# Attention on one core: casts and the normalising product read PSUM, V is made ahead of the denominators, and two of a step's four maxima move ahead of its value products

## The chip, the core and the metric

The program runs on one core of a Trainium2 chip. Its engines are TensorE (PE, matmuls; PEld is its weight load), VectorE (DVE), ScalarE (ACT) and GpSimd (POOL), with SyncE (SP) issuing DMAs; they run independently and wait for each other by semaphores. SBUF is the working memory; PSUM, where matmuls write, has 8 banks of 128 x 512 f32. The metric is the device time of one execution in microseconds; the time of a kernel is the median of its runs.

## The reference, cut to the part that is changed

The whole program is a layer norm, an attention block, a feed-forward block with two convolutions, a whitening and a state-space block, on an input of 16 images of 64 channels and 32 x 32 points. Only the attention is changed:

```python
qkv = x_ln @ w_qkv.T                              # x_ln: 16 images x 1024 points x 64
q, k, v = (to_heads(t) for t in jnp.split(qkv, 3, axis=-1))     # 8 heads of 32
scores = jnp.einsum('bhqd,bhkd->bhqk', q, k) * HEAD_DIM ** (-0.5)
attn = jax.nn.softmax(scores, axis=-1)
out = jnp.einsum('bhqk,bhkd->bhqd', attn, v)
```

## The kernel before

The attention goes through 32 periods: 16 images, each with two groups of four heads. A period has 16 steps, s = 0 to 15, in two halves of eight: the half picks 512 queries, and the step within it, kb = 0 to 7, picks 128 keys. The order on each engine is written out by hand (`period` in each engine's block), with semaphores between engines. An engine takes its own list in that order.

In a step PE makes the scores of four heads (L402, into the four banks `at_sc`) and subtracts each query's maximum with a one-row matmul (L409). ACT turns them into `at_probs` in two exponentials of two heads each (L510). PE multiplies them by V into the single bank `at_O` (`values`, L421; the table `PV_AT` says in which step which blocks are multiplied). POOL adds the probabilities up over kb (L607, five additions per half, and one block by DMA, L602), and PE turns the sums into denominators in `at_O` (`denominator`, L385). ACT takes Ln and Exp(-x) of them (`reciprocal`, L482 and L486), and DVE multiplies the raw output by that (`normalise`, L568).

The maxima for the softmax are made ahead, by a second, cheaper product of bf16 copies of q and k (`QH`, `KH`): four matmuls per step, one per head (`maxima`, L341), each into one bank of the ring `at_ring`, and DVE reduces each over its 512 keys (`reduce`, L548). The ring has three banks (`SLOTS`), dealt out in turn. A fourth kind of unit also uses the ring: `extra` says in which step q or k of the next period is projected (`project`, L354; q in steps 0 and 9, k in 1 and 3) or the maxima are turned into a row (`turn`, L379; steps 7 and 15). The unit that gets a bank waits until the one three places before it in the ring's order has been taken out (`wait_for_bank`). So the fourth maximum of a step waits for the reduction of the first of the same step, or of the second where an extra unit stands between.

For q and k, ACT takes the projection from the ring to SBUF (`take`, L469), and DVE casts that copy to bf16 (`cast`, L563), both in SBUF, after the reductions of the step. V of the next period is projected into `at_O` (`values_projected`, L369) in step kb = 3, after the reciprocal has read it, and taken by ACT (L490). The waits stand in the order in which PE meets them:

```python
scores(stage, grp, par, s)
maxima(stage, grp, par, s, (0, 1))
# kb == 2: denominators_added, denominators_sums;  kb == 3: values_projected
for k in PV_AT.get(kb, ()): ...            # values
for kind, which in extra.get(s, []): ...   # turn or project
maxima(stage, grp, par, s, (2, 3))
```

Of the kernel before, what the change touches and what calls it, by code (L numbers as in the profile page):

```python
# [11 lines left out]
P = 128  # L12
# [135 lines left out]
def attention_phase(nc, sem, xn_d, wqkvT, ident_bf, attn_d):  # L148
# [73 lines left out]
    with ExitStack() as ctx:  # L222
# [18 lines left out]
        rden = sb("at_rden", [P, HALF])  # L241
# [79 lines left out]
        def _(pe):  # L321
# [35 lines left out]
            def values_projected(stage, grp, par, half):  # L357
                if stage == "last":
                    return
                if stage == "lead" or (stage == "first" and half == 0):  # L360
                    if v_halves(grp, half) > 1:
                        pe.wait_ge(v_done, v_halves(grp, half) - 1)
                else:
                    pe.wait_ge(lden_done, 2 * grp + half)
                at = 2 * INNER + (1 - par) * P
                rows = slice(half * C, (half + 1) * C)
                for n in range(KB // 2):
                    k = half * KB // 2 + n
                    m = nc.tensor.matmul(O[:, blk(n)], xn[rows, blk(k)], w[rows, at:at + P], start=True, stop=True)  # L369
                m.then_inc(v_ready, 1)  # L370
# [17 lines left out]
            def denominators_added(of_half):  # L388
                pe.wait_ge(raw_done, of_half + 1)
# [21 lines left out]

            def values(stage, grp, par, half, kb):
                if kb == 0:
                    if stage == "last":
                        pe.wait_ge(lden_done, 2 * grp + half)
                    else:
                        pe.wait_ge(v_done, v_halves(grp, half))
                if kb == KB - 1:
                    pe.wait_ge(exp_done, 2 * (STEPS * grp + KB * half + kb) + 2)
                for h in range(GH):  # L420
                    m = nc.tensor.matmul(O[head(h), :], V[:, par, kb, head(h)], probs[:, kb, h, :],  # L421
                                         start=(kb == 0), stop=(kb == KB - 1))
                m.then_inc(pv_done, 1)
# [4 lines left out]
            def period(grp, par, stage):  # L428
                for s in range(STEPS):
                    half, kb = divmod(s, KB)  # L430
                    closes = stage != "lead" and not (stage == "first" and half == 0)
                    was_grp, was_par, was_half = half_before(grp, par, half)
                    if stage != "lead":
                        scores(stage, grp, par, s)
                    maxima(stage, grp, par, s, (0, 1))
                    if closes and kb == ADDED_AT:
                        denominators_added(2 * grp + half - 1)
                    if closes and kb == SUMS_AT:
                        denominators_sums(2 * grp + half - 1, was_half)
                    if kb == V_AT:  # L440
                        values_projected(stage, grp, par, half)
                    if stage != "lead":
# [5 lines left out]
                    for kind, which in extra.get(s, []):  # L448
                        if kind == "turn":
                            turn(stage, grp, which)  # L450
                        else:
                            project(stage, grp, par, kind, which)
                    maxima(stage, grp, par, s, (2, 3))
                if stage == "last":
                    values(stage, grp, par, 1, KB - 1)
                    denominators_added(2 * NG - 1)
                    denominators_sums(2 * NG - 1, 1)

            pe.wait_ge(xn_in, 2 * DMA)
# [4 lines left out]
        def _(act):  # L464
            nc.scalar.preload_act_table_set("natural_log_exp_and_others")

            def take(stage, grp, unit, to):
                act.wait_ge(extra_ready, unit_count(stage, grp, unit))
                nc.scalar.activation(to, ring[:, unit[3], :], ACT.Copy).then_inc(extra_done, 1)  # L469

            def take_raw(grp, half):
# [5 lines left out]
            def reciprocal(of_half):  # L477
# [6 lines left out]
                if not first:  # L484
                    act.wait_ge(od_free, of_half)
# [7 lines left out]
            def period(grp, par, stage):  # L493
                for s in range(STEPS):
# [17 lines left out]
                                                 scale=SCALE).then_inc(exp_done, 1)  # L512
                    if closes and kb == 0:
                        take_raw(grp if half else grp - 1, 1 - half)
                    if closes and kb == SUMS_AT:
                        reciprocal(2 * grp + half - 1)
                    if stage != "last" and kb == V_AT:
                        take_v(grp, par, half)
# [16 lines left out]
        def _(dve):  # L535
# [22 lines left out]
            def cast(stage, grp, par, kind, which):  # L558
                if not executed(stage, kind, which, which):
                    return  # L560
                of, to = {"q": (QT, QH), "k": (KT, KH)}[kind]
                dve.wait_ge(extra_done, unit_count(stage, grp, unit_of(stage, kind, which)))
                nc.vector.tensor_copy(to[:, 1 - par, hs(which)], of[:, 1 - par, hs(which)]).then_inc(cast_done, 1)  # L563

            def normalise(grp, half):
                dve.wait_ge(raw_done, 2 * grp + half + 1)
                dve.wait_ge(rden_done, 2 * grp + half + 1)
                nc.vector.tensor_tensor(att[:, half, :], att[:, half, :], rden[:], ALU.mult).then_inc(od_free, 1)  # L568

            def period(grp, par, stage):  # L570
                for s in range(STEPS):
                    reduce(stage, grp, s, (0, 1))
                    if s == 3 and stage not in ("lead", "first"):
                        normalise(grp - 1, 1)
                    if s == KB + 3 and stage != "lead":
                        normalise(grp, 0)
                    reduce(stage, grp, s, (2, 3))
                    for kind, which in extra.get(s, []):
                        if kind in MADE_AHEAD:
                            cast(stage, grp, par, kind, which)  # L580
                    if s == LATE - 1:
                        combine(stage, grp, s, 1)
                    if s == LATE + KB - 1:
# [1184 lines left out]
```

## Time and profile before

| | |
|---|---|
| median of 3 runs | 3789.77 us (3788.62 to 3790.57) |
| the profiled execution: its own time, its span | 3794.89 us, 3793.2 us |
| mean granted TensorE clock | 0.911 of full |
| busy of the span: PE, DVE, ACT, POOL | 86%, 73%, 54%, 60% |
| DVE reductions of the maxima (L548) | 2048, 1289.7 us |
| POOL additions of the probabilities (L607) | 320, 1451.3 us |
| ACT exponentials (L510) | 1024, 992.8 us |

The attention takes more than half of the span, and nothing outside it is changed. In its stretch PE looks busy nearly all the time, so the lengths of steps and the waits between matmuls say more than busy shares. A row of a timeline gives the start, the duration (of the whole group, if several instructions were merged), the engine, the line, what is written and read, the count, and in brackets the idle time before it and what ended it. Starts of PE rows are exact; their ends are modelled.

### The profile page before, as it was taken

Reading aid. Unit: us, or ns where it says so; the run is one execution under the profiler, and the core shown is the slowest. Engines: PE = TensorE matmul, PEld = TensorE weight load, DVE = VectorE, ACT = ScalarE, POOL = GpSimd, SP = SyncE. Lnnn points to the kernel's source line nnn. Section 1 sums busy time; section 2 is a strip of 40 time slices with the busy share of each in tenths; the row PEclk is TensorE's granted clock in tenths of the full one; section 3 lists DMA queues with packets and bytes.
Section 4 is the critical chain, followed back from the end, with each engine's and each line's share of the span. In section 5 each row is a group of like instructions: output and inputs, shape, how many; then the busy total and the mean of one; then the engine's idle time right before and its main releaser. Section 6 shows DMA issues by size and latency. Waiting matters only on the chain. (4 is left out here: it accounts for less than half of the span.)

```text
span 3793.2 us, 55116 instructions
## 1 busy us (share of the span) xinstructions
PE 3248.7 (86%) x18038; PEld 1243.0 (33%) x18038; DVE 2753.4 (73%) x3346; ACT 2046.5 (54%) x2445; POOL 2269.8 (60%) x748
## 2 busy tenths in 40 slices
PE   6999999999989999999999599955688887888887
PEld 2333333333333333333333133342222222222322
DVE  5788878888778888787885122223788888888888
ACT  3566666666656666666666233323556455455464
POOL 0677777777767777777777200001666666667666
PEclk7799999999989999999999799977898999999999
DMA  2121222122212221222212411013443344434433
GB/s 99 34 51 44 55 48 48 43 49 48 48 43 48 48 48 43 48 49 51 48 43 48 127 67 72 11 58 107 146 150 139 118 143 151 134 119 148 150 136 121
DMA packets 83956, 301.94 MB, mean 80 GB/s; under 512 B 14112, under 2 KB 15204, under 8 KB 75444
## 3 DMA queue, kind: packets, MB, share of 16 engines
q1 hardware_dynamic: 69460, 215.06, 16.9%
q0 software_dynamic: 14272, 83.94, 10.0%
q8 instruction: 135, 2.21, 0.2%
q14 instruction: 89, 0.73, 0.1%
HBM read 192.42 MB, written 39.39 MB: 61 GB/s over the span
## 5 line engine op out<-in xcount | busy, mean ns | idle before, releaser
L548 DVE TENSOR_REDUCE at_pmax<-at_ring 128x1 f32<-128x512 f32 x2048 | 1289.7, 683 | 378.7 <-PE at_ring L341 377.5
L607 POOL TENSOR_TENSOR at_prob_sums<-at_prob_sums,at_probs 128x2048 f32<-128x2048 f32 x256 | 1161.1, 4535 | 394.0 <-ACT at_probs L510 383.1
L510 ACT ACTIVATE at_probs<-at_sc 128x1024 f32<-128x1024 f32 x1024 | 992.8, 1021 | 701.1 <-PE at_sc L409 698.1
L1661 POOL TENSOR_TENSOR ss_drive<-ss_du,ss_bsb 128x1024 f32<-128x1024 f32 x261 | 610.9, 2353 | 270.9 <-DVE ss_state L1618 263.2
L402 PE MATMUL at_sc<-at_QT,at_KT 32*128 32x512 f32 x4096 | 765.4, 677 | 7.4 <-issue 5.3
L341 PE MATMUL at_ring<-at_KH,at_QH 32*128 32x512 bf16 x2048 | 490.6, 406 | 124.8 <-DVE at_pmax L548 120.6
L1561 ACT ACTIVATE ss_decay<-ss_delta,ss_a 128x512 f32<-128x512 f32 x520 | 354.4, 687 | 447.3 <-DVE ss_state L1614 301.3
L421 PE MATMUL at_O<-at_probs,at_V 128*32 128x512 f32 x4096 | 530.0, 626 | 1.1 <-ACT at_probs L510 1.1
L1450 PE MATMUL ss_Y<-ss_seen,ss_ident 128*128 128x512 f32 x1032 | 524.1, 632 | 0.0
L1626 DVE TENSOR_TENSOR ss_seen<-ss_state,ss_C 128x1024 f32<-128x1024 f32 x259 | 316.2, 1221 | 87.5 <-PE ss_C L1438 79.6
L341 PEld LDWEIGHTS at_ring<-at_KH,at_QH 32*128 32x128 bf16 x2048 | 149.0, 95 | 678.3 <-DVE at_pmax L548 445.4
L607 POOL TENSOR_TENSOR at_prob_sums<-at_probs 128x2048 f32<-128x2048 f32 x64 | 290.2, 4534 | 119.4 <-ACT at_probs L510 119.4
L1618 DVE TENSOR_TENSOR_SCAN ss_state<-ss_decay,ss_state,ss_drive 128x512 f32<-128x512 f32 x259 | 332.2, 1283 | 31.5
L1614 DVE TENSOR_TENSOR_SCAN ss_state<-ss_decay,ss_drive 128x512 f32<-128x512 f32 x259 | 314.8, 1216 | 32.4 <-POOL ss_drive L1661 16.5
L1438 PE MATMUL ss_C<-ss_bc,ss_select 96*128 96x512 bf16 x518 | 163.6, 399 | 188.9 <-DVE ss_seen L1626 188.5
L409 PE MATMUL at_sc<-at_nrow,at_ones_bf 1*128 1x512 bf16 x2048 | 307.5, 401 | 0.1
L1450 PEld LDWEIGHTS ss_Y<-ss_seen,ss_ident 128*128 128x128 f32 x1032 | 204.8, 203 | 233.0 <-issue 197.2
L402 PEld LDWEIGHTS at_sc<-at_QT,at_KT 32*128 32x128 f32 x4096 | 253.1, 194 | 21.8 <-ACT at_probs L510 11.0
L965 POOL DMA_DIRECT2D scratch_x<-fc_out x8 | 4.3, 534 | 353.4 <-ACT fc_out L866 353.4
L354 PE MATMUL at_ring<-at_xn,at_w 64*128 64x512 f32 x256 | 166.3, 742 | 31.5 <-DMA at_xn<-scratch_xn 19.6
L421 PEld LDWEIGHTS at_O<-at_probs,at_V 128*32 128x32 f32 x4096 | 103.7, 112 | 249.0 <-issue 247.0
L1438 PEld LDWEIGHTS ss_C<-ss_bc,ss_select 96*128 96x128 bf16 x518 | 40.5, 101 | 383.2 <-DVE ss_seen L1626 318.6
(196 smaller groups left out, 3069.2 us busy)
## 6 DMA issues: line engine op xcount, KB each, us to landing
ss_bsb<-scratch_rows SPq DMA_DIRECT2D x265, 512.0 KB, 7.1
at_probs<-at_probs POOLq DMA_DIRECT2D x64, 1024.0 KB, 7.0
scratch_attn<-at_att SPq DMA_DIRECT2D x64, 256.0 KB, 2.0
fc_att<-scratch_attn SPq DMA_DIRECT2D x32, 512.0 KB, 5.6
ss_xn<-scratch_xm SPq DMA_DIRECT2D x34, 256.0 KB, 5.7
at_xn<-scratch_xn SPq DMA_DIRECT2D x32, 256.0 KB, 3.8
ss_xw<-scratch_xw SPq DMA_DIRECT2D x17, 256.0 KB, 3.8
ln_x<-in_x SPq DMA_DIRECT2D x8, 512.0 KB, 4.3
```

The costliest lines, as they stand in the source:

```text
L341: nc.tensor.matmul(ring[:, unit[3], :], QH[head(h), p, blk(quad // 2)], KH[head(h), p, hs(quad % 2)], start=True, stop=True).then_inc(max_ ...
L402: nc.tensor.matmul(sc[:, h, :], KT[head(h), par, blk(kb)], QT[head(h), par, hs(half)], start=True, stop=False)
L421: m = nc.tensor.matmul(O[head(h), :], V[:, par, kb, head(h)], probs[:, kb, h, :], start=(kb == 0), stop=(kb == KB - 1))
L510: nc.scalar.activation(probs[:, kb, two, :].rearrange("p h q -> p (h q)"), sc[:, two, :].rearrange("p h q -> p (h q)"), ACT.Exp, scale=SCA ...
L548: nc.vector.tensor_reduce(pmax[:, quad // 2, h, quad % 2:quad % 2 + 1], ring[:, unit[3], :], AX_X, ALU.max, negate=True).then_inc(max_done, 1)
L607: nc.gpsimd.tensor_tensor(prob_sums[:, half, :, :], before, probs[:, k, :, :], ALU.add).then_inc(pool_sums, 1)
L1450: m = nc.tensor.matmul(Y[:, hs(h)], ident[:], seen[:, n % DEPTH, hs(h)], start=False, stop=(n == N - 1))
L1561: nc.scalar.activation(decay[:, hs(h)], delta[:, par, hs(h)], ACT.Exp, scale=a_neg[:, n:n + 1])\
L1614: nc.vector.tensor_tensor_scan(now[:, hs(0)], decay[:, hs(0)], drive[:, n % DEPTH, hs(0)], 0.0, ALU.mult, ALU.add).then_inc(first_half_don ...
L1618: nc.vector.tensor_tensor_scan(now[:, hs(1)], decay[:, hs(1)], drive[:, n % DEPTH, hs(1)], now[:, HALF - 1:HALF], ALU.mult, ALU.add).then_ ...
L1626: nc.vector.tensor_tensor(seen[:, n % DEPTH, :], state[:, n % 2, :], Cp[:], ALU.mult).then_inc(seen_done, 1)
L1661: nc.gpsimd.tensor_tensor(drive[:, n % DEPTH, :], du[:, par, :], bsb[:, n % SLOTS, :], ALU.mult).then_inc(drive_done, 1)
```

## The change

Five things are done together, all in the attention:

- `cast` reads the projection from the ring in PSUM, where it read ACT's copy in SBUF. It waits for PE alone, and stands between the reductions of heads 0 and 1 and those of heads 2 and 3 of its step. ACT's `take` of q and k now waits for the cast, so that the bank is given back after both.
- The reciprocal's Exp writes `at_O` in place of an SBUF tile `rden`, and `normalise` reads it from there. It stands ahead of all four reductions of kb = 3, where it stood between the second and the third.
- V is projected in kb = 1, right after the raw output has been taken, and the denominators of kb = 2 wait until ACT has taken V.
- The first block of value products waits for `normalise` and goes into kb = 3. `PV_AT` has 1, 2, 2, 1, 1 blocks in kb = 3 to 7, and before had 2, 2, 2, 1 in kb = 4 to 7.
- On PE, projections, turns and the maxima of heads 2 and 3 come ahead of the step's value products, where they came behind them.

```diff
-    ADDED_AT, SUMS_AT, V_AT = 2, 2, 3
+    V_AT, SUMS_AT = 1, 2
-    PV_AT = {0: (LAST_KB,), 4: (0, 1), 5: (2, 3), 6: (4, 5), 7: (6,)}
+    PV_AT = {0: (LAST_KB,), 3: (0,), 4: (1, 2), 5: (3, 4), 6: (5,), 7: (6,)}
...
-                    pe.wait_ge(lden_done, 2 * grp + half)
+                    pe.wait_ge(raw_done, 2 * grp + half)
...
-                    if stage == "last":
-                        pe.wait_ge(lden_done, 2 * grp + half)
+                    if stage == "first" and half == 0:
+                        pe.wait_ge(v_done, v_halves(grp, half))
                     else:
-                        pe.wait_ge(v_done, v_halves(grp, half))
+                        pe.wait_ge(od_free, 2 * grp + half)
...
+                if unit[1] in MADE_AHEAD:
+                    act.wait_ge(cast_done, casts(grp, *unit[1:3]))
                 nc.scalar.activation(to, ring[:, unit[3], :], ACT.Copy).then_inc(extra_done, 1)
...
-                nc.scalar.activation(rden[:], lden[:], ACT.Exp, scale=-1.0).then_inc(rden_done, 1)
+                nc.scalar.activation(O[:], lden[:], ACT.Exp, scale=-1.0).then_inc(rden_done, 1)
...
-                dve.wait_ge(extra_done, unit_count(stage, grp, unit_of(stage, kind, which)))
-                nc.vector.tensor_copy(to[:, 1 - par, hs(which)], of[:, 1 - par, hs(which)]).then_inc(cast_done, 1)
+                dve.wait_ge(extra_ready, unit_count(stage, grp, unit))
+                nc.vector.tensor_copy(to[:, 1 - par, hs(which)], ring[:, unit[3], :]).then_inc(cast_done, 1)
...
-                nc.vector.tensor_tensor(att[:, half, :], att[:, half, :], rden[:], ALU.mult).then_inc(od_free, 1)
+                nc.vector.tensor_tensor(att[:, half, :], att[:, half, :], O[:], ALU.mult).then_inc(od_free, 1)
```

On PE, a step with two blocks of value products (kb = 5), before: `at_max_done` is the reductions' semaphore, `at_cast_done` the casts', and x8 value products are two blocks of four heads.

```order
L341 MATMUL at_ring<-at_KH,at_QH 128x512 [waits at_max_done,at_cast_done]
L341 MATMUL at_ring<-at_KH,at_QH 128x512 [waits at_max_done]
L421 MATMUL at_O<-at_probs,at_V 32x512 x8
L341 MATMUL at_ring<-at_KH,at_QH 128x512 [waits at_max_done] x2
L402 MATMUL at_sc<-at_QT,at_KT 128x512 [waits at_exp_done]
```

The same place after:

```order
L340 MATMUL at_ring<-at_KH,at_QH 128x512 [waits at_max_done,at_cast_done]
L340 MATMUL at_ring<-at_KH,at_QH 128x512 [waits at_max_done] x3
L423 MATMUL at_O<-at_probs,at_V 32x512 x8
L404 MATMUL at_sc<-at_QT,at_KT 128x512 [waits at_exp_done]
L404 MATMUL at_sc<-at_QT,at_KT 128x512
```

The value products stood between the second and the third maximum; all four maxima now stand in a row ahead of them, and the next scores follow the value products.

On DVE, from the second reduction of step 0 to the cast of step 1 (the register rows set a wait's count), before:

```order
L548 TENSOR_REDUCE at_pmax<-at_ring 128x1 [waits at_max_ready]
L562 ISA
L563 CAST at_QH<-at_QT 128x512 [waits at_extra_done]
L547 REGISTER_ALU
L548 TENSOR_REDUCE at_pmax<-at_ring 128x1 [waits at_max_ready]
L547 REGISTER_ALU
L548 TENSOR_REDUCE at_pmax<-at_ring 128x1 [waits at_max_ready]
```

After:

```order
L550 TENSOR_REDUCE at_pmax<-at_ring 128x1 [waits at_max_ready]
L565 ISA
L566 CAST at_QH<-at_ring 128x512 [waits at_extra_ready]
L549 REGISTER_ALU
L550 TENSOR_REDUCE at_pmax<-at_ring 128x1 [waits at_max_ready]
L549 REGISTER_ALU
L550 TENSOR_REDUCE at_pmax<-at_ring 128x1 [waits at_max_ready]
```

The cast before follows the fourth reduction of its step and waits for ACT's copy; after, it follows the second, and waits for the projection itself.

## Rows read from the trace of the kernel before

**Rows 1.** L475 by source: instructions, shortest, median, longest ns, first and last start.

```profile
L475 ACT ACTIVATE at_att<-at_O x64: 597/597/603, 136.7 to 2090.0; 128x512 f32<-128x512 f32 x64
```

**Rows 2.** Windows: length, busy by engine (instructions), granted clock, DMA share, GB/s.

```profile
90.00:2100.00 2010.00, 1859.63 (x14278) 727.00 (x14278) 1586.26 (x2268) 1239.46 (x1466) 1504.95 (x384) 0.92 0.21 47
```

**Rows 3.** Timeline of PE, a step with two blocks of value products.

```profile
802.58 1.24 PE L402 MATMUL at_sc<-at_QT,at_KT 32*128 32x512 f32 x8
...
803.76 0.38 PE L341 MATMUL at_ring<-at_KH,at_QH 32*128 32x512 bf16 x2
804.07 1.92 PE L421 MATMUL at_O<-at_probs,at_V 128*32 128x512 f32 x16
805.92 0.39 PE L341 MATMUL at_ring<-at_KH,at_QH 32*128 32x512 bf16 x2
```

**Rows 4.** Timeline of DVE behind those maxima.

```profile
806.35 2.48 DVE L548 TENSOR_REDUCE at_pmax<-at_ring 128x1 f32<-128x512 f32 x4 [0.64 <-PE at_ring L341]
```

**Rows 5.** Timeline of PE, the one block of value products of step 8.

```profile
814.51 1.07 PE L421 MATMUL at_O<-at_probs,at_V 128*32 128x512 f32 x8
815.51 0.39 PE L341 MATMUL at_ring<-at_KH,at_QH 32*128 32x512 bf16 x2
```

**Rows 6.** Timeline of PE from the denominators of step 10 to the scores of step 13.

```profile
820.16 1.06 PE L385 MATMUL at_O<-at_probs,at_ones 128*32 128x512 f32 x8
...
822.02 0.39 PE L341 MATMUL at_ring<-at_KH,at_QH 32*128 32x512 bf16 x1
824.39 0.39 PE L341 MATMUL at_ring<-at_KH,at_QH 32*128 32x512 bf16 x1 [1.98 <-DVE at_pmax L548]
824.48 1.24 PE L402 MATMUL at_sc<-at_QT,at_KT 32*128 32x512 f32 x8
...
827.57 2.36 PE L402 MATMUL at_sc<-at_QT,at_KT 32*128 32x512 f32 x8
...
833.68 1.24 PE L402 MATMUL at_sc<-at_QT,at_KT 32*128 32x512 f32 x8
```

**Rows 7.** Timeline of DVE and of POOL: the casts and what POOL runs.

```profile
819.96 3.77 DVE L563 CAST at_QH<-at_QT 128x512 bf16<-128x512 f32 x1
823.65 3.71 DVE L548 TENSOR_REDUCE at_pmax<-at_ring 128x1 f32<-128x512 f32 x6
...
863.90 0.42 DVE L563 CAST at_KH<-at_KT 128x512 bf16<-128x512 f32 x1
...
818.91 4.53 POOL L607 TENSOR_TENSOR at_prob_sums<-at_probs 128x2048 f32<-128x2048 f32 x1 [0.38 <-ACT at_probs L510]
```

**Rows 8.** Windows of 2 us in the slow step 12.

```profile
829.00:831.00 2.00, 2.00 (x16) 0.37 (x12) 1.31 (x3) 0.89 (x1) 0.00 (x0) 0.50 0.35 131
```

**Rows 9.** Waits of 90 to 2100 us: in total, times, longest.

```profile
PE at_ring L341 <- DVE at_pmax L548: 118.3, 96, 2.0
```

**Rows 10.** Timeline of PE: V projected and a projection of q, each with its follower.

```profile
394.86 1.16 PE L369 MATMUL at_O<-at_w,at_xn 64*128 64x128 f32 x8
395.95 0.39 PE L341 MATMUL at_ring<-at_KH,at_QH 32*128 32x512 bf16 x2
...
846.61 1.12 PE L354 MATMUL at_ring<-at_xn,at_w 64*128 64x512 f32 x2
847.67 0.39 PE L341 MATMUL at_ring<-at_KH,at_QH 32*128 32x512 bf16 x2
```

**Rows 11.** Timeline of ACT: the reciprocal of step 10.

```profile
822.15 0.60 ACT L482 ACTIVATE at_lden<-at_O 128x512 f32<-128x512 f32 x1 [0.27 <-PE at_O L385]
822.78 0.63 ACT L486 ACTIVATE at_rden<-at_lden 128x512 f32<-128x512 f32 x1
```

**Rows 12.** By source, as rows 1: DVE products, and the reductions.

```profile
L568 DVE TENSOR_TENSOR at_att<-at_att,at_rden x64: 680/1367/3471, 148.0 to 2097.2; 128x512 f32<-128x512 f32 x64
L1626 DVE TENSOR_TENSOR ss_seen<-ss_state,ss_C x259: 1220/1221/1222, 2677.4 to 3787.9; 128x1024 f32<-128x1024 f32 x130
L548 DVE TENSOR_REDUCE at_pmax<-at_ring x2048: 673/681/694, 67.0 to 2049.0; 128x1 f32<-128x512 f32 x187
```

More of the change, by code:

```diff
@@ L386, in denominator, with denominators_added @@
                 return m
-            def denominators_added(of_half):
-                pe.wait_ge(raw_done, of_half + 1)
+            def denominators_added(of_half, v_count):
+                if v_count is None:
+                    pe.wait_ge(raw_done, of_half + 1)
+                else:
+                    pe.wait_ge(v_done, v_count)
                 pe.wait_ge(block_added, DMA * (of_half + 1))
@@ L435, in period @@
                     maxima(stage, grp, par, s, (0, 1))
[L436 to L439, printed above, removed]
                     if kb == V_AT:
                         values_projected(stage, grp, par, half)
+                    if closes and kb == SUMS_AT:
+                        denominators_added(2 * grp + half - 1, None if stage == "last" else v_halves(grp, half))
+                        denominators_sums(2 * grp + half - 1, was_half)
+                    for kind, which in extra.get(s, []):
+                        if kind != "turn":
+                            project(stage, grp, par, kind, which)
+                    for kind, which in extra.get(s, []):
+                        if kind == "turn":
+                            turn(stage, grp, which)
+                    maxima(stage, grp, par, s, (2, 3))
                     if stage != "lead":
@@ L447, in period @@
                                 values(stage, was_grp, was_par, was_half, k)
[L448 to L453, printed above, removed]
                 if stage == "last":
                     values(stage, grp, par, 1, KB - 1)
-                    denominators_added(2 * NG - 1)
+                    denominators_added(2 * NG - 1, None)
                     denominators_sums(2 * NG - 1, 1)
@@ L483, in reciprocal @@
                 act.wait_ge(lden_done, of_half + 1)
-                if not first:
-                    act.wait_ge(od_free, of_half)
-                nc.scalar.activation(rden[:], lden[:], ACT.Exp, scale=-1.0).then_inc(rden_done, 1)
+                nc.scalar.activation(O[:], lden[:], ACT.Exp, scale=-1.0).then_inc(rden_done, 1)
             def take_v(grp, par, half):
@@ L514, in period @@
                         take_raw(grp if half else grp - 1, 1 - half)
+                    if stage != "last" and kb == V_AT:
+                        take_v(grp, par, half)
                     if closes and kb == SUMS_AT:
                         reciprocal(2 * grp + half - 1)
-                    if stage != "last" and kb == V_AT:
-                        take_v(grp, par, half)
                     for kind, which in extra.get(s, []):
@@ L560, in cast @@
                     return
-                of, to = {"q": (QT, QH), "k": (KT, KH)}[kind]
-                dve.wait_ge(extra_done, unit_count(stage, grp, unit_of(stage, kind, which)))
-                nc.vector.tensor_copy(to[:, 1 - par, hs(which)], of[:, 1 - par, hs(which)]).then_inc(cast_done, 1)
+                to = {"q": QH, "k": KH}[kind]
+                unit = unit_of(stage, kind, which)
+                dve.wait_ge(extra_ready, unit_count(stage, grp, unit))
+                nc.vector.tensor_copy(to[:, 1 - par, hs(which)], ring[:, unit[3], :]).then_inc(cast_done, 1)
             def normalise(grp, half):
@@ L567, in normalise @@
                 dve.wait_ge(rden_done, 2 * grp + half + 1)
-                nc.vector.tensor_tensor(att[:, half, :], att[:, half, :], rden[:], ALU.mult).then_inc(od_free, 1)
+                nc.vector.tensor_tensor(att[:, half, :], att[:, half, :], O[:], ALU.mult).then_inc(od_free, 1)
             def period(grp, par, stage):
                 for s in range(STEPS):
+                    if s == SUMS_AT + 1 and stage not in ("lead", "first"):
+                        normalise(grp - 1, 1)
+                    if s == KB + SUMS_AT + 1 and stage != "lead":
+                        normalise(grp, 0)
                     reduce(stage, grp, s, (0, 1))
[L573 to L577, printed above, removed]
                     for kind, which in extra.get(s, []):
@@ L580, in period @@
                             cast(stage, grp, par, kind, which)
+                    reduce(stage, grp, s, (2, 3))
                     if s == LATE - 1:
```

1 line of the change is left out of this document (removed).

## The prediction, made before the changed kernel had run

> **What bounds the kernel now.** I read the length of a half first: ACT takes the raw output once per half, 64 times from 136.7 to 2090.0 [rows 1], so a half lasts (2090.0 - 136.7) / 63 = 31.0 us. Then the steps in PE's timeline. In an undisturbed step with two blocks of value products the scores start at 802.58, the maxima 1.18 us later, the value products 1.49 us later, and the next maxima and scores at 805.92 [rows 3]: 3.34 us, with PE never idle. DVE is through four maxima in 2.48 us and then waits for PE [rows 4]. Such steps are bound by PE.
>
> Two places per period are not. In step 10 the fourth maximum starts 1.98 us late, behind a reduction [rows 6], because DVE stood in a cast of 3.77 us [rows 7]. The same cast takes 0.42 us with POOL idle; here POOL was inside its addition of 4.53 us [rows 7]. So the cast waits for POOL, DVE for the cast, and PE for DVE. Over the attention PE waits 118 us in this way [rows 9]. Behind the long wait the granted clock falls to 0.50, the 1.2 GHz level [rows 8], and a step with two blocks takes 833.68 - 827.57 = 6.11 us [rows 6], which is 2.8 us more than 3.34. The mean clock of 0.92 over 2010 us [rows 2] makes 2 x 0.08 x 2010 = 322 us at the lower level, a loss of at most half of that, 161 us. All that the casts can give back is thus 118 + 161 = 279 us.
>
> **Casts, product and V.** The trace has no cast from PSUM. Its bounds are 0.42 and 3.77 us [rows 7]; the nearest row is the reduction of the same 512 numbers of PSUM, 0.673 to 0.694 us in all 2048 cases, POOL busy or not [rows 12]. I take 0.68, so the wait of 1.98 us goes. The Trainium skill ("VectorE: DVE Perf Modes", section "Why PSUM operands drop a tier") says that a PSUM operand costs a copy its faster mode, and its cycle table gives an estimate of (120 + 512) / 0.96 GHz = 0.66 us; no run here shows it, and with 0.66 the sum would be some 2 us lower. A cast at 0.42 us would save 0.26 us in three steps per period, some 25 us.
>
> The product took 0.68 us or, next to POOL, 1.37 [rows 12]. With one PSUM operand the nearest row is the product of the state-space block, 1.22 us for twice the columns in all 259 cases, with POOL at work beside it [rows 12]; I take 0.68. At 1.37 each half would be 0.7 us longer, 43 us in all.
>
> ACT's copy of q and k now waits for the cast, and behind it on ACT stand the next step's exponentials. In kb = 1 the projection ends 3.6 us into the step, the cast 0.7 and the copy 0.6 us later (a copy of ACT takes 0.6 us [rows 1]), 1.2 us into the next step; its scores are not complete before that, since its maxima follow them at 1.18 [rows 3]. So nothing is lost on ACT, and what the bank's late return costs on PE is counted below at kb = 1 and 2.
>
> V costs PE 395.95 - 394.86 = 1.09 us [rows 10] wherever it stands. It waits for the raw output, which ACT has taken 0.6 us [rows 1] after the last value product of kb = 0, while PE is still at the scores of kb = 1: no wait. The denominators, 822.02 - 820.16 = 1.86 us [rows 6], find V taken. SP's loads and stores wait for the same events, and POOL's order is unchanged.
>
> **The maxima ahead of the value products.** This is the term that decides. The ring has three banks, so the fourth maximum of a step waits for the reduction of the first. Before, the value products stood between and hid that. Now nothing does. From the start of a step's scores: first maximum at 1.18, over 0.38 later [rows 3]; DVE starts 0.06 later (a maximum ends at 805.92 + 0.39, DVE starts at 806.35 [rows 3, 4]); one reduction 0.68 [rows 12]; PE 0.06 later (the reduction ends at 823.65 + 0.68, the maximum starts at 824.39 [rows 6, 7]). The fourth maximum starts at 2.36. PE does not pass it: at 824.39 the scores behind it, whose own inputs were ready, started only 0.09 us after the released maximum [rows 6]. The value products come 0.31 later (804.07 - 803.76 [rows 3]), at 2.67; two blocks take 1.86 [rows 3], one block 1.00 (815.51 - 814.51 [rows 5]). Where a turn or projection stands between, the wait is for the second reduction, 0.60 later ((2.48 - 0.68) / 3 [rows 4]). New lengths of steps:
>
> - kb = 4 and 5, two blocks: 2.67 + 1.86 = 4.53 each. kb = 6, one block: 3.67. kb = 7, one block and a turn: 4.27.
> - kb = 0: 3.67, or 4.27 in the first half, with q's projection.
> - kb = 1: 1.49 + 1.09 (V) + 1.06 (projection, 847.67 - 846.61 [rows 10]) = 3.65; 0.1 more in the first half, where the bank of q comes free only after cast and take.
> - kb = 2: 1.49 + 1.86, and about 0.2 for the same reason = 3.55.
> - kb = 3: DVE still has two reductions of kb = 2 until about 1.7 us into the step, then the product (its reciprocal, 0.60 + 0.63 [rows 11], is ready by 1.4), then the first reduction: 1.7 + 0.68 + 0.68 + 0.06 = 3.14, values at 3.45, end at 4.45. With k's projection in the first half, 0.60 more: 5.05.
>
> The second half sums to 3.67 + 3.65 + 3.55 + 4.45 + 4.53 + 4.53 + 3.67 + 4.27 = 32.32, the first to 4.27 + 3.75 + 3.55 + 5.05 + 4.53 + 4.53 + 3.67 + 4.27 = 33.62; the mean is 32.97, against 31.0 now, which has its waits and slow stretches in it. Over 62 halves (the last period makes no maxima for a next) that is 1.97 x 62 = +122 us. POOL's five additions of 4.53 us and ACT's work fit into 33 us.
>
> This sum is at full clock. The longest wait left is that of kb = 3, 3.14 - 1.49 = 1.65 us in the second half and about 1.2 in the first, where k's projection fills some; the others are 0.9 or less. The wait before the present fall was 1.98 us. Stretches at the lower level last some 7 us now, so 322 us are about 46 of them; with the waits shorter I count 25, at 2.8 us each (the slow step): 70 us. Bounds are 0, and one per half, 174 us.
>
> **The sum.** The profiled execution took 3794.89 us, 5 over the median of 3789.77. 3794.9 + 122 + 70 - 5 = 3982, rounded to 3980: slower by 5%. An error of 0.25 us in the six steps with a wait moves it by 93 us.
>
> **Rivals.** (1) Faster: the value products do not in fact stand behind the waiting maximum, or the maxima come sooner than DVE's rows allow, so that only the gain is left: 3790 - 279 = 3510. For it: DVE is idle 0.64 us before its four reductions [rows 4], so earlier maxima feed it. Against it: the scores at 824.48 did stand behind. It decides for faster once the waits come out more than (122 + 70) / 62 = 3.1 us per half shorter than I sum them. Chance 0.15.
> (2) The clock stays at 2.4 GHz: 3982 - 70 = 3912. For it: the longest wait is cut. The Trainium skill ("TensorE: Matmul & The Clock Gate", Part 1) has the clock fall after the engine has been idle and come back with sustained work; by it alone, shorter waits would leave it up, while the row shows it falling behind 1.98 us with work on both sides. Chance 0.20.
> (3) It falls in every half, since PE is now idle for 0.9 us or so in most steps as well: 3912 + 174 = 4086. Chance 0.14.
> (4) No change: gain and waits cancel, near 3790. Chance 0.04.
>
> **How the numbers follow.** The forecast, 3980, has 0.47, with a range of its own from 3870 to 4090. Slower by over 0.2% (about what a measurement of this kernel can tell from no change) is 0.47 + 0.20 + 0.14 = 0.81, the same 0.04, faster 0.15. The range from 3790 to 4110 takes in (2), (3) and (4) with the error of the steps, and leaves out the faster case and a little at the top.
>
> **What would show it.** In the changed profile: casts of about 0.68 us with no case of 3 us; a step kb = 4 or 5 of 4.5 us, with the fourth maximum idle for 0.7 to 1 us behind a reduction; the total of PE's waits for reductions well above 118 us in place of near zero; DVE idle between the fourth reduction and the next step. I am wrong if steps with two blocks stay near 3.4 us, if the casts still take 3.7 us, or if the mean clock in the attention goes above 0.97 and the time still rises past 4000.

## The result, and the profile after

The changed kernel takes 3904.87 us (median of 3 runs, 3893.07 to 3906.3) against 3789.77: a ratio of 1.0295, 95% interval 1.0264 to 1.0326, slower by 3%. The forecast was 3980, so the sign was right and the size 75 us too large. Nearest is the rival with TensorE's clock at its upper level, 3912.

| | before | after |
|---|---|---|
| the profiled execution: its own time, its span | 3794.89, 3793.2 us | 3904.87, 3903.2 us |
| mean granted clock, whole span | 0.911 | 0.940 |
| length of a half in the attention | 31.0 us [rows 1] | (2206.1 - 146.2) / 63 = 32.7 us |
| PE's waits for reductions in the attention | 118.3 us, 96 times [rows 9] | 250.2 us, 441 times |
| busy of the span: PE, DVE | 86%, 73% | 83%, 65% |

The halves carry the loss: (32.7 - 31.0) x 63 = 107 us of the 110 us between the two spans. The source view of the raw output's copy gives their length, as [rows 1] did before:

```profile
L479 ACT ACTIVATE at_att<-at_O x64: 597/597/605, 146.2 to 2206.1; 128x512 f32<-128x512 f32 x64
```

PE's timeline of the changed kernel, a step with two blocks of value products (start, duration, line, tiles, count, idle time before and what ended it), answers to [rows 3]:

```profile
813.68 1.15 PE L404 MATMUL at_sc<-at_QT,at_KT 32*128 32x512 f32 x8
...
814.86 0.39 PE L340 MATMUL at_ring<-at_KH,at_QH 32*128 32x512 bf16 x3
816.02 0.39 PE L340 MATMUL at_ring<-at_KH,at_QH 32*128 32x512 bf16 x1 [0.77 <-DVE at_pmax L550]
816.34 1.92 PE L423 MATMUL at_O<-at_probs,at_V 128*32 128x512 f32 x16
818.19 1.15 PE L404 MATMUL at_sc<-at_QT,at_KT 32*128 32x512 f32 x8
```

The step lasts 818.19 - 813.68 = 4.51 us, where it lasted 3.34. Of the 1.17 us, 0.77 are PE's wait for the reduction that frees the ring's bank, and 0.40 are the two maxima themselves: before, the last two started at 805.92 [rows 3], together with the next scores, and cost nothing of their own; now the scores come only after the value products. The scores' row of before:

```profile
805.93 1.24 PE L402 MATMUL at_sc<-at_QT,at_KT 32*128 32x512 f32 x8
```

DVE's timeline of the same stretch shows the other side. It is through the four reductions in 2.48 us, as in [rows 4], and is then idle for some 2 us, where it was idle 0.64:

```profile
815.27 2.49 DVE L550 TENSOR_REDUCE at_pmax<-at_ring 128x1 f32<-128x512 f32 x4 [1.76 <-PE at_ring L340]
819.79 2.48 DVE L550 TENSOR_REDUCE at_pmax<-at_ring 128x1 f32<-128x512 f32 x4 [2.03 <-PE at_ring L340]
```

The waits between 90 and 2220 us (in total, times, longest) put this together: each engine waits for the other, again and again. In a period without disturbance PE waits for a reduction in eleven of the sixteen steps, and in eight of these once for some 0.77 us.

```profile
PE at_ring L340 <- DVE at_pmax L550: 250.2, 441, 1.4
...
DVE at_pmax L550 <- PE at_ring L340: 665.6, 441, 5.8
```

What the change took away is gone. The groups of DVE between 90 and 2220 us (busy, mean ns, idle before) have all casts and products at 0.68 to 0.69 us, where casts took up to 3.77 [rows 7] and products up to 3.47 [rows 12]:

```profile
L571 DVE TENSOR_TENSOR at_att<-at_att,at_O 128x512 f32<-128x512 f32 x64 | 43.4, 678 | 47.3 <-ACT at_O L488 47.3
L566 DVE CAST at_QH<-at_ring 128x512 bf16<-128x512 f32 x62 | 42.6, 687 | 11.4 <-PE at_ring L353 11.4
L566 DVE CAST at_KH<-at_ring 128x512 bf16<-128x512 f32 x62 | 42.6, 686 | 15.6 <-PE at_ring L353 15.6
```

And TensorE's clock rose. The window over the attention, with the columns of [rows 2], grants 0.97, which makes 2 x 0.03 x 2130 = 128 us at the lower level in place of 322. (Both figures take in the opening of the window, which stands at 0.50 in either kernel: the first 41 us after, the first 33 before.)

```profile
90.00:2220.00 2130.00, 1855.39 (x14283) 591.25 (x14282) 1384.36 (x2279) 1239.26 (x1467) 1503.41 (x386) 0.97 0.20 44
90.00:131.00 41.00, 39.38 (x149) 12.14 (x151) 24.89 (x42) 12.68 (x15) 13.51 (x3) 0.50 0.00 1
131.00:2200.00 2069.00, 1807.22 (x14085) 577.46 (x14079) 1357.70 (x2230) 1219.63 (x1444) 1478.55 (x378) 0.98 0.20 45
```

### The profile page after: what moved, and what is told of

Same layout as the page of the kernel before. It is cut to its first block and busy times, and to the rows that moved or that the text cites. A ratio compares the mean times of both kernels' runs of the same rounds, so it can differ in the third digit from the quotient of the medians.

```text
span 3903.2 us, 55181 instructions
## 1 busy us (share of the span) xinstructions
PE 3237.2 (83%) x18038; PEld 1105.2 (28%) x18038; DVE 2548.8 (65%) x3346; ACT 2044.9 (52%) x2445; POOL 2267.0 (58%) x748
## 5 line engine op out<-in xcount | busy, mean ns | idle before, releaser
L404 PE MATMUL at_sc<-at_QT,at_KT 32*128 32x512 f32 x4096 | 627.1, 651 | 3.4 <-issue 2.9
L340 PEld LDWEIGHTS at_ring<-at_KH,at_QH 32*128 32x128 bf16 x2048 | 129.1, 93 | 788.7 <-DVE at_pmax L550 589.0
L404 PEld LDWEIGHTS at_sc<-at_QT,at_KT 32*128 32x128 f32 x4096 | 187.4, 187 | 335.5 <-issue 239.0
L411 PE MATMUL at_sc<-at_nrow,at_ones_bf 1*128 1x512 bf16 x2048 | 231.7, 383 | 0.0
L353 PE MATMUL at_ring<-at_xn,at_w 64*128 64x512 f32 x256 | 152.2, 676 | 26.7 <-DMA at_xn<-scratch_xn 19.3
L423 PEld LDWEIGHTS at_O<-at_probs,at_V 128*32 128x32 f32 x4096 | 94.9, 109 | 173.8 <-issue 164.0
```

The costliest lines, as they stand in the source:

```text
L340: nc.tensor.matmul(ring[:, unit[3], :], QH[head(h), p, blk(quad // 2)], KH[head(h), p, hs(quad % 2)], start=True, stop=True).then_inc(max_ ...
L404: nc.tensor.matmul(sc[:, h, :], KT[head(h), par, blk(kb)], QT[head(h), par, hs(half)], start=True, stop=False)
```

## The experiments

The theory was that two things of opposite sign are mixed: the reads of PSUM gain, and the place of maxima 2 and 3 ahead of the value products loses more, through the three banks of the ring. The rivals were that the reads gain nothing here, that V's early place matters, and that the granted clock moves the time rather than the waits. Each kernel was timed beside the kernel before on the same chip (3790.28 us for the first four below, 3781.12 for the product alone and for the last kernel, 3781.64 for the rest); ratios are to that, with 95% intervals.

**Order, undone.** Everything of the change stays, but the value products go back to where they stood, ahead of projections, turns and maxima 2 and 3.

```diff
+                    if stage != "lead": ...        # values of this step
                     for kind, which in extra.get(s, []): ...   # project, turn
                     maxima(stage, grp, par, s, (2, 3))
-                    if stage != "lead": ...        # values of this step
```

> The changed kernel with the value products back between the maxima of heads 0 and 1 and the projection, turn and maxima of heads 2 and 3; casts and product in PSUM, V in kb = 1 and the value products in kb = 3 to 7 stay. Bank theory (the loss is the wait of the fourth maximum for its ring bank, 0.8 us and more in twelve steps per period): the idle time of 0.77 us ahead of the fourth maximum is gone, steps of two blocks take 3.35 us, a half some 27 us, the time is 3,550 us (3,510 to 3,600). Rival (the loss is in the other parts, the chain of product, V and first value block through the one bank at_O): the time stays above 3,790 us.

Measured: 3581.67 us (3575.72 to 3583.55), ratio 0.9454 (0.9426 to 0.9482). The bank theory held. One piece of order is worth 3905 - 3582 = 323 us. PE's timeline of this kernel:

```profile
810.02 1.24 PE L404 MATMUL at_sc<-at_QT,at_KT 32*128 32x512 f32 x8
...
811.51 1.92 PE L423 MATMUL at_O<-at_probs,at_V 128*32 128x512 f32 x16
813.37 0.39 PE L340 MATMUL at_ring<-at_KH,at_QH 32*128 32x512 bf16 x2
813.37 1.24 PE L404 MATMUL at_sc<-at_QT,at_KT 32*128 32x512 f32 x8
```

The step is back at 813.37 - 810.02 = 3.35 us, without a wait, and the last two maxima start with the next scores. PE's one sizeable wait in the attention is a new one, for the product, ahead of the first block of value products:

```profile
PE at_O L423 <- DVE at_att L571: 49.9, 63, 0.9
```

**Only the fourth maximum.** The changed kernel with maximum 2 left ahead of the value products and maximum 3 put behind them.

```diff
-                    maxima(stage, grp, par, s, (2, 3))
+                    maxima(stage, grp, par, s, (2,))
                     if stage != "lead": ...        # values of this step
+                    maxima(stage, grp, par, s, (3,))
```

> The changed kernel with only the fourth maximum (head 3) moved behind the value products; the third, projections and turns stay ahead. Bank theory: only this one waits for a bank filled in the same step, so nearly all of the loss goes: 3,560 us (3,520 to 3,620), with 0.45 us of waiting left in the steps with a turn, where the third maximum waits for the first. Rival (any maximum ahead of the value products costs): above 3,700 us.

Measured: 3596.98 us (3596.01 to 3601.16), ratio 0.95 (0.9473 to 0.9527). It held too. Of the 323 us, 308 come back with this single matmul per step. It is the one that finds the ring's three banks taken by the three before it. So the bank is the cause of nearly all of the loss, and not that matmuls were moved as such.

**Order, alone.** The kernel before, with only PE's order changed.

```diff
-                    if stage != "lead": ...        # values of this step
                     for kind, which in extra.get(s, []): ...   # turn, project
                     maxima(stage, grp, par, s, (2, 3))
+                    if stage != "lead": ...        # values of this step
```

> The kernel before with only PE's order changed: projections, turns and the maxima of heads 2 and 3 ahead of a step's value products (blocks still 2, 2, 2, 1 in kb = 4 to 7), casts in SBUF. Bank theory: 1.16 us more in three steps of two blocks, 1.2 us more in kb = 7 and 0.3 in kb = 0 of each half, 4.9 us per half, so 3,790 + 62 x 4.9 = 4,095 us (4,040 to 4,160); the waits behind casts and the low clock stay, clock about 0.92. Rival (the order costs little): under 3,850 us.

Measured: 4201.37 us (4196.6 to 4217.8), ratio 1.1105 (1.1066 to 1.1145). Right in sign, but some 110 us above the forecast. The undisturbed steps are 4.51 us as in the changed kernel; what was underrated is the clock, which falls to 0.87 over the attention: 2 x 0.13 x 2430 = 632 us at the lower level. Its window, and PE's waits in it:

```profile
90.00:2520.00 2430.00, 2089.97 (x14279) 709.97 (x14278) 1598.76 (x2274) 1242.06 (x1467) 1506.14 (x385) 0.87 0.17 39
```

```profile
PE at_ring L341 <- DVE at_pmax L548: 321.9, 421, 2.5
```

**Casts, alone.** The kernel before, with only the casts reading PSUM.

```diff
+                if unit[1] in MADE_AHEAD:
+                    act.wait_ge(cast_done, casts(grp, *unit[1:3]))
...
-                nc.vector.tensor_copy(to[:, 1 - par, hs(which)], of[:, 1 - par, hs(which)]).then_inc(cast_done, 1)
+                nc.vector.tensor_copy(to[:, 1 - par, hs(which)], ring[:, unit[3], :]).then_inc(cast_done, 1)
```

> The kernel before with only the casts read from PSUM, between the second and the third reduction. Bank theory: the casts take 0.69 us, PE's waits for reductions fall from 118 us to under 40 us, the granted clock of the attention rises from 0.92 to 0.97, and the time is 3,555 us (3,520 to 3,620): nearly the whole gain of the first run. Rival (the gain needs the product and V too): 3,650 to 3,750 us, with the wait in kb = 3 left, where DVE's product reads SBUF next to POOL.

Measured: 3814.39 us (3812.21 to 3843.5), ratio 1.0086 (1.0055 to 1.0118). A clear miss: no gain at all, a small loss. The groups of DVE show why:

```profile
L571 DVE TENSOR_TENSOR at_att<-at_att,at_rden 128x512 f32<-128x512 f32 x63 | 219.1, 3477 | 18.9 <-ACT at_rden L488 18.9
L566 DVE CAST at_QH<-at_ring 128x512 bf16<-128x512 f32 x62 | 42.8, 691 | 24.9 <-PE at_ring L354 24.4
L566 DVE CAST at_KH<-at_ring 128x512 bf16<-128x512 f32 x62 | 42.4, 684 | 3.5 <-PE at_ring L354 3.1
```

The casts are at 0.69, and the product now takes 3.48 us on the mean. DVE comes to it earlier, since no cast holds it up, and so meets POOL's addition some 1.3 to 1.6 us after its start; most of the products that waited in the kernel before met it 3.75 us after. One case, from the timelines of DVE and of POOL:

```profile
807.73 3.42 DVE L571 TENSOR_TENSOR at_att<-at_att,at_rden 128x512 f32<-128x512 f32 x1
...
806.10 4.51 POOL L610 TENSOR_TENSOR at_prob_sums<-at_prob_sums,at_probs 128x2048 f32<-128x2048 f32 x1
```

POOL ends at 806.10 + 4.51 = 810.61, the product 0.54 us later, at 811.15: it did its work only when POOL had ended. Behind the product stands the cast of k, behind that ACT's copy, which in this kernel waits for the cast, and PE waits 2.81 us for the bank:

```profile
812.44 0.68 PE L341 MATMUL at_ring<-at_KH,at_QH 32*128 32x512 bf16 x2 [2.81 <-ACT at_KT L471]
```

**Product, alone.** The other half: Exp writes the bank and the product reads it, ahead of the four reductions; V and the value products of kb = 0 wait for it. The casts stay in SBUF.

```diff
-                nc.scalar.activation(rden[:], lden[:], ACT.Exp, scale=-1.0).then_inc(rden_done, 1)
+                nc.scalar.activation(O[:], lden[:], ACT.Exp, scale=-1.0).then_inc(rden_done, 1)
...
-                nc.vector.tensor_tensor(att[:, half, :], att[:, half, :], rden[:], ALU.mult).then_inc(od_free, 1)
+                nc.vector.tensor_tensor(att[:, half, :], att[:, half, :], O[:], ALU.mult).then_inc(od_free, 1)
```

> The kernel before with the product alone reading PSUM (Exp writes the bank, the product stands ahead of the four reductions, V and the value products of kb = 0 wait for it); the casts stay in SBUF behind the fourth reduction. Theory, that the waits on POOL form a chain and moving one operation to PSUM leaves the other to wait: casts still of 3.5 us and more, PE's wait of some 2 us behind them stays, attention clock 0.91 to 0.93, 3,750 us (3,720 to 3,790). Rival, that each of the two gives its share of the 216 us that both gave together: 3,680 us (3,650 to 3,700). Rival, that the product is the whole cause: about 3,570.

Measured: 3836.62 us (3816.58 to 3837.91), ratio 1.0131 (1.0098 to 1.0163). No rival's gain, and more than the theory gave: slower by 1.3%. The product is at 0.67 us, and the casts are where they were (2.20 and 2.00 us on the mean for q and k, 2.20 and 2.02 before). PE's timeline has the stall of [rows 6] unchanged and a second wait close behind it, for the product:

```profile
843.73 0.38 PE L340 MATMUL at_ring<-at_KH,at_QH 32*128 32x512 bf16 x1 [1.98 <-DVE at_pmax L545]
...
846.11 2.07 PE L368 MATMUL at_O<-at_w,at_xn 64*128 64x128 f32 x8 [0.48 <-DVE at_att L565]
```

The clock over the attention is 0.89, below the 0.92 of before. Why the second wait, of 25.7 us in all, goes with a lower clock isn't shown.

**Casts and product, nothing else.** Both reads of PSUM in the kernel before; V stays in kb = 3, behind the product, and PE's order and the table of value products stay as they were. Its edit is that of the two kernels above together, with the cast between the reductions of heads 1 and 2.

> The kernel before with casts and product from PSUM, and nothing else moved on PE: V stays in kb = 3, and has to wait for the product, which reads the bank that V is written to; value products stay 2, 2, 2, 1 in kb = 4 to 7. Theory that the two reads of PSUM are the whole gain and V's place is worth little: casts and products of 0.69 us, clock 0.97, 3,590 us (3,550 to 3,640). Rival (V ahead carries a part of the gain): above 3,650 us.

Measured: 3565.83 us (3561.61 to 3573.19), ratio 0.9436 (0.9416 to 0.9455). It held. Alone the two reads cost 0.9% and 1.3%; together they gain 5.6%, 216 us. With the casts alone in PSUM, the wait for POOL moves to the product and grows; with the product alone in PSUM, it stays with the casts. Only when neither operation reads two SBUF operands or casts within SBUF does it leave the chain. This kernel has V and the value products in their old places and is not slower than the first one (0.9436 against 0.9454, the intervals overlap): V's early place, together with the new table of value products, is worth nothing that shows. PE's waits:

```profile
PE at_O L368 <- DVE at_att L568: 48.3, 61, 0.8
...
PE at_ring L340 <- DVE at_pmax L547: 3.4, 6, 1.4
```

**The changed kernel with its casts back in SBUF.** They stand behind the fourth reduction again, and ACT's copy no longer waits for them.

```diff
-                nc.vector.tensor_copy(to[:, 1 - par, hs(which)], ring[:, unit[3], :]).then_inc(cast_done, 1)
+                nc.vector.tensor_copy(to[:, 1 - par, hs(which)], of[:, 1 - par, hs(which)]).then_inc(cast_done, 1)
```

> The changed kernel with the casts alone put back: they read ACT's copy in SBUF, behind the fourth reduction; the order of PE, product, V and value products stay changed. Theory that the falls of the clock belong to the waits behind casts: PE's longest waits of 2 us are back, the mean granted clock of the attention goes from 0.97 to about 0.91, and the time to 4,060 us (3,980 to 4,150). Rival (the waits of 0.8 us at the maxima and the shape of the steps set the clock, the casts do not): clock 0.96 or more and 3,905 to 3,980 us.

Measured: 4198.41 us (4188.12 to 4200.71), ratio 1.1104 (1.1085 to 1.1122). The direction held, the size did not: 4198 - 3905 = 293 us for the casts, with the clock at 0.88 where 0.91 was expected. With the old order the same step is worth 3837 - 3566 = 271 us (the product alone against both reads), so the casts cost about as much under either order.

**The wait made longer.** To separate the wait from the clock, the fourth maximum of the changed kernel waits for one reduction more, in the steps without projection or turn.

```diff
+                    later = unit[1:3] == ("max", 3) and before[2][:3] == (unit[0], "max", 0)
-                    pe.wait_ge(max_done if before[2][1] == "max" else extra_done, unit_count(*before))
+                    pe.wait_ge(max_done if before[2][1] == "max" else extra_done, unit_count(*before) + later)
```

> The changed kernel, in which the fourth maximum of a step without turn or projection waits for one reduction more (the second instead of the first), and nothing else is different: a wait of 0.77 us becomes one of 1.37 us in eight steps per period. Bank theory: 8 x 0.6 x 31 = 149 us more, 4,054 us (4,010 to 4,100) if the clock stays at 0.97. If waits of 1.4 us are enough to bring the clock down: clock under 0.95 and more than 4,120 us. Rival (the wait is hidden by something else): under 3,950 us.

Measured: 4305.37 us (4274.34 to 4344.11), ratio 1.1377 (1.1288 to 1.1465). PE's timeline, and windows of 5 us in it with the granted clock as the third number from the end:

```profile
1264.85 1.15 PE L405 MATMUL at_sc<-at_QT,at_KT 32*128 32x512 f32 x8
...
1267.79 0.38 PE L341 MATMUL at_ring<-at_KH,at_QH 32*128 32x512 bf16 x1 [1.36 <-DVE at_pmax L551]
...
1269.95 1.15 PE L405 MATMUL at_sc<-at_QT,at_KT 32*128 32x512 f32 x8
...
1280.65 2.10 PE L405 MATMUL at_sc<-at_QT,at_KT 32*128 32x512 f32 x8
```

```profile
1265.00:1270.00 5.00, 3.64 (x36) 0.95 (x36) 2.48 (x4) 1.94 (x2) 2.82 (x2) 1.00 0.00 0
1275.00:1280.00 5.00, 4.77 (x28) 1.07 (x20) 2.58 (x4) 2.43 (x3) 4.05 (x2) 0.50 0.28 57
```

The wait is 1.36 us in place of 0.77 and the step 1269.95 - 1264.85 = 5.10 us, 0.6 more, as it had to be. Shortly after, the clock is at 0.50, the 1.2 GHz level. Over the attention it is 0.86. The profiled execution took 4280.3 us, and its span is 4278.6 - 3903.2 = 375 us longer than the changed kernel's. Of these the waits themselves make only 393 - 250 = 143; the rest came with the clock. The periods say the same: six of 31 last some 69.5 us, which is the undisturbed 64.77 of the changed kernel and eight times 0.6, and the slowest take 88.7.

**Projection first.** The first kernel again (value products ahead of turn and maxima 2 and 3), with the projections left ahead of the value products.

```diff
                     for kind, which in extra.get(s, []): ...   # project
+                    if stage != "lead": ...        # values of this step
                     for kind, which in extra.get(s, []): ...   # turn
                     maxima(stage, grp, par, s, (2, 3))
-                    if stage != "lead": ...        # values of this step
```

> The kernel of the first run (value products ahead of the maxima of heads 2 and 3) with the projections moved ahead of the value products, as in the changed kernel; turns and maxima stay behind. In kb = 3 of the first half the projection of k, 1.06 us, fills the 0.79 us that PE waits there for the product, and casts and banks come free earlier in kb = 0, 1 and 4: 1.2 us less per period, 3,545 us (3,520 to 3,585). Rival (the projection ahead delays what ACT and DVE wait for): 3,582 us or more.

Measured: 3539.88 us (3534.18 to 3543.7), ratio 0.9358 (0.934 to 0.9376). It held. The projection covers the wait for the product in one of two halves:

```profile
PE at_O L423 <- DVE at_att L571: 25.3, 32, 0.8
```

The same in the kernel with V in its old place, the projection ahead of V:

```diff
+                    for kind, which in extra.get(s, []): ...   # project
                     if kb == V_AT:
                         values_projected(stage, grp, par, half)
                     if stage != "lead": ...        # values of this step
-                    for kind, which in extra.get(s, []): ...   # turn, project
+                    for kind, which in extra.get(s, []): ...   # turn
```

> The kernel before with casts and product reading PSUM, V left in kb = 3, and one change of order: a projection stands ahead of V and of the step's value products; turns and the maxima of heads 2 and 3 stay behind them. Theory, that a projection ahead covers the wait for the product, as it gave 42 us in the version with V ahead: 3,525 us (3,505 to 3,545), with half of the 61 waits of 0.8 us for the product gone. Rival, that V in kb = 3 covers the same time already: 3,566 us (3,555 to 3,575), no gain.

Measured: 3530.86 us (3528.7 to 3538.03), ratio 0.9345 (0.9326 to 0.9364). It held. The wait for the product is down from 61 times to 31. This has the lowest median of all, though its interval overlaps that of the kernel above: the kernel before with two reads of PSUM and one move of order. Both gains, of some 35 to 42 us, are more than the 24 us of waits that went; where the rest came from isn't shown.

```profile
PE at_O L368 <- DVE at_att L569: 24.6, 31, 0.8
```

## Why the prediction was right in sign, and where it was too high

**The bank of the ring: right.** The chain to the fourth maximum was put at 2.36 us into the step; it starts at 816.02 - 813.68 = 2.34. (DVE's start behind a maximum, put at 0.06, is 806.35 - 806.31 = 0.04 by the rows it was read from.) The wait of 0.77 us lies in the 0.7 to 1 us named, and nothing behind it passes it. The first two experiments on the order show that this is nearly all of the loss, 308 of 323 us.

**The steps at full clock: 36 us too many.** The mean half was put at 32.97 us; an undisturbed period measures 64.77 us, a half 32.39, and two thirds of the periods are undisturbed. The scores of step 0 of two periods in a row:

```profile
826.10 1.15 PE L404 MATMUL at_sc<-at_QT,at_KT 32*128 32x512 f32 x8
...
890.87 1.15 PE L404 MATMUL at_sc<-at_QT,at_KT 32*128 32x512 f32 x8
```

So the steps cost (32.39 - 31.0) x 62 = 86 us, not 122. Forecast and measured, in us:

| step | first half | second half |
|---|---|---|
| kb = 0 | 4.27, 4.25 | 3.67, 3.65 |
| kb = 1 | 3.75, 3.29 | 3.65, 3.11 |
| kb = 2 | 3.55, 3.74 | 3.55, 3.74 |
| kb = 3 | 5.05, 4.87 | 4.45, 4.27 |
| kb = 4 and 5 | 4.53, 4.51 | 4.53, 4.51 |
| kb = 6 | 3.67, 3.65 | 3.67, 3.65 |
| kb = 7 | 4.27, 4.25 | 4.27, 4.25 |

Two terms failed. In kb = 1, V and the projection were added up, 1.09 + 1.06 us; they run into each other on PE. The changed kernel's timeline there:

```profile
864.32 0.82 PE L368 MATMUL at_O<-at_w,at_xn 64*128 64x128 f32 x5
864.87 0.69 PE L353 MATMUL at_ring<-at_xn,at_w 64*128 64x512 f32 x1
864.98 0.50 PE L368 MATMUL at_O<-at_w,at_xn 64*128 64x128 f32 x3
865.40 0.59 PE L353 MATMUL at_ring<-at_xn,at_w 64*128 64x512 f32 x1
865.93 0.39 PE L340 MATMUL at_ring<-at_KH,at_QH 32*128 32x512 bf16 x2
```

The projection's first matmul starts before V's last three, and both together take 865.93 - 864.32 = 1.61 us, not 2.15. [rows 10] were taken from places where each stood alone; a place of before where the one follows the other shows it: there a projection starts at 860.05 and V's last three matmuls at 860.26. In kb = 3, product and reduction were put in a row with their durations, 0.68 each (and the four terms of that sum make 3.12, not 3.14). The product starts 1.62 us into that step, as forecast by 1.7, but behind it the next operation of DVE starts 0.60 later, not 0.68, which was in [rows 4] and was used in other steps only. These two are too long by some 1.4 us per period; kb = 2, where the bank comes back later than I thought, is too short by 0.4.

**The clock: 46 us too many, the largest miss.** The sum had 25 stretches at the lower level, 70 us. The spans differ by 110 us, 86 of which are the steps, so the rest is 24. The stretches were counted by guess between 0 and one per half, although the one fall in the rows stood behind 1.98 us; the trace has 10 in place of the 25, 72 us in all. The runs give the ground for a better count. In the table, low us is twice the missing clock times the length of the window (0.005 of rounding makes 20 us of it, and the opening some 33 to 41); falls are the stretches at the lower level that begin between 135 us and the last copy of raw output, in the trace's record of the granted clock:

| kernel | clock in the attention | low us | falls, us in all | PE's waits for reductions: total, longest |
|---|---|---|---|---|
| changed | 0.97 | 128 | 10, 72 | 250.2, 1.4 |
| changed, wait longer | 0.86 | 703 | 52, 645 | 392.6, 1.4 |
| changed, casts in SBUF | 0.88 | 583 | 65, 546 | 353.9, 2.0 |
| before, order alone | 0.87 | 632 | 64, 567 | 321.9, 2.5 |
| before | 0.92 | 322 | 39, 276 | 118.3, 2.0 |
| before, casts alone | 0.92 | 326 | 62, 280 | 80.2, 2.5; for ACT's copy behind the cast 82.3, 3.0 |
| before, product alone | 0.89 | 449 | 55, 399 | 116.9, 2.0; for the product 25.7, 0.8 |
| before, casts and product | 0.98 | 75 | 4, 20 | 3.4, 1.4; for the product 48.3, 0.8 |

The total of the waits doesn't set the clock: before had less waiting and a lower clock than after. Waits of 0.77 us in eight of sixteen steps left it up, 1.36 us in the same steps did not, and each kernel that often waits for 2 us or more has it low. Casts from SBUF go with 39 falls under the old order and with 64 or 65 under the new, whose steps have waits of their own, and there a fall also lasts longer, 8.4 to 8.9 us on the mean against 7.1. So the price of the clock is both more falls and longer ones. What makes the clock fall in one period and not in the next isn't shown.

The Trainium skill ("TensorE: Matmul & The Clock Gate", Part 1) has the clock follow how busy the engine has lately been. The traces agree as far as idle time goes; they show it falling with work on both sides of waits of 1.4 to 2 us.

**Casts and product: right in price, wrong in what they give back.** 0.68 was taken for both; measured are 0.69 and 0.678. The estimate of 0.66 for the cast, from the cycle table of the Trainium skill's "VectorE: DVE Perf Modes" (section "The TRN2 errata"), was 0.03 lower than the trace. But the working ascribed all the 118 us of waits and 161 us of slow clock to the casts. The 161 us are at most 138: of the 322 us at the lower level, only 276 lie in falls behind the opening. And the two one-sided kernels show that neither read has a gain of its own. There was a hint of it in [rows 12]: a product of up to 3.471 us stood there, and I read its median. The best kernel gains 3781 - 3531 = 250 us, near the 279 named as the most, but with one more move of order. The section "Who interferes with whom" in the Trainium skill's "SBUF — State Buffer" has a VectorE instruction with two SBUF inputs contend with a GpSimd instruction that reads SBUF, and one in a two-port mode and GpSimd block each other for a whole instruction. The traces agree: the product above ends 0.54 us after POOL's addition, and the cast of [rows 7] ends at 819.96 + 3.77 = 823.73, 0.29 us after POOL's end at 823.44. That the cast runs in a two-port mode, no run here shows.

**The rivals.** The faster one (3510, chance 0.15) needed the value products not to stand behind the waiting maximum. They do stand there, in each step that has value products and such a wait. Its figure is what the change without its order is near to: 3531 to 3582. The rival with the clock at its upper level gave 3912, 7 us from the measured time, by luck: the clock did fall, for some 24 us, and the 36 us too many in its steps made up for that. That the clock falls in every half is out, with 10 falls in 62 halves.

## What to carry to other kernels

Before an instruction that waits for a buffer is moved ahead of work that waits for nothing, count the buffers: with three banks and four units the fourth has to have independent work in front of it, and one such matmul per step cost 308 us here. When one engine's operations are held up by another engine's, move all of them, since the wait goes to the next one left: each of two cures alone cost 1%, both together gained 5.6%. And take a wait's price with the clock in mind: 0.6 us more in half of the steps turned a loss of 3% into one of 14%.

## What the runs showed of the hardware that was not expected

- The granted clock stayed at 0.97 with a wait of 0.77 us in eight of a period's sixteen steps, and went to 0.86 with 1.36 us in the same steps.
- A product of 0.68 us that reads SBUF twice and meets POOL's addition ended some 0.55 us after it, however long it had been waiting by then: 44 cases in the kernel before, most of them of 1.37 us, and 62 with the casts alone in PSUM, of 3.4 to 3.7 us. The same product with one operand in PSUM took 677 to 689 ns in all 64 cases, 63 of them with POOL's addition beside it.
- V's matmuls and those of a projection, 64 rows each, ran into each other on PE: 1.61 us for both, where one alone takes 1.09 and the other 1.06.
